# Query chunks of 512 columns with convolutions beside them, and 65-column arrays in a four-layer convolution and state-space network

## The reference

```python
# layer 0 (xf is the input plus its frequency-gated copy)
x_flat = xf.reshape(b, c, n).transpose(0, 2, 1)
q = (x_flat @ q_w + q_b)...                      # queries of all n pixels
xs = _conv(xf, sr_w, stride) + sr_b              # 8x8 stride 8, and 16x16 stride 16
...                                              # keys, values, attention, + x
# layer 2, its end
y = gaussian_smoothing_4d(dht_2d(out_ht) / (H * W))
mask = (jnp.abs(jnp.fft.fftfreq(W)) <= 0.25)     # 65 of 128 columns stay
return y * mask
# layer 3
xs = x.transpose(0, 2, 3, 1).reshape(1, -1, C)   # one sequence over all pixels
ys = mamba_fwd(xs, spa_...)                      # spatial branch
xe = x.transpose(0, 2, 3, 1).reshape(B * H * W, TOKEN, gcn)
ye = mamba_fwd(xe, spe_...)                      # spectral branch, each pixel by itself
spa = silu(group_norm(ys, ...)) + x
spe = x + silu(group_norm(ye, ...))
return spa * w[0] + spe * w[1] + x
```

## Time and profile before

| what | us |
|---|---|
| median of 3 runs (7890.61 to 7903.71) | 7898.19 |
| the profiled execution, device time | 7902.44 |
| its span | 7900.3 |
| patch stage, first load to the next stage's first load | 496.0 to 823.0 |
| attention | 893 to 2180 |
| spatial stage, first load of x to last result | 3547 to 5591 |
| spectral stage, first load of x to last result | 5601 to 7663 |
| merge stage | 7669 to 7900 |

### The profile page before, as it was taken

One profiled execution on the slowest core, in us unless ns is written; L12 is line 12 of the kernel. 1 busy time (PEld: TensorE's weight loads), 2 busy tenths in 40 slices (PEclk: granted clock), 3 DMA queues, 4 the chain that ended last, 5 costly groups with the idle time before them and its releaser, 6 DMA issues. The chain is left out here.

```text
span 7900.3 us, 122279 instructions
## 1 busy us (share of the span) xinstructions
PE 6835.9 (87%) x38266; PEld 3658.0 (46%) x38266; DVE 5843.1 (74%) x5708; ACT 4011.5 (51%) x6797; POOL 3601.8 (46%) x2430
## 2 busy tenths in 40 slices
PE   8967699999965499778999999999899999999970
PEld 7842333333244145662222222222477777777750
DVE  4652577777613385018999999999799999999975
ACT  4423366666612474015666666666455555555532
POOL 0100122222202000006777777777687787787860
PEclk9988799999977798668999999999899999999985
DMA  2252234334357333440000000000000000000016
GB/s 70 69 174 103 58 99 99 99 99 100 92 124 236 129 101 116 120 65 14 14 14 14 13 15 13 13 15 9 15 11 10 10 10 11 9 10 10 10 40 188
DMA packets 560486, 478.16 MB, mean 61 GB/s; under 512 B 181789, under 2 KB 486851, under 8 KB 551771
## 3 DMA queue, kind: packets, MB, share of 16 engines
q1 hardware_dynamic: 560155, 473.52, 21.9%
HBM read 306.97 MB, written 163.76 MB: 60 GB/s over the span
## 5 line engine op out<-in xcount | busy, mean ns | idle before, releaser
L2657 POOL TENSOR_TENSOR spe_hc<-spe_hs,spe_cu 128x1024 f32<-128x1024 f32 x552 | 1291.3, 2359 | 312.0 <-DVE spe_hs L2854 312.0
L2253 POOL TENSOR_TENSOR spa_hc<-spa_hs,spa_cr 128x966 f32<-128x966 f32 x592 | 1224.2, 2068 | 426.5 <-DVE spa_hs L2527 410.4
L2527 DVE TENSOR_TENSOR_SCAN spa_hs<-spa_p_d,spa_hs,spa_bx 128x483 f32<-128x483 f32 x1168 | 1359.4, 1204 | 0.0
L2854 DVE TENSOR_TENSOR_SCAN spe_hs<-spe_p_d,spe_bx 128x1024 f32<-128x1024 f32 x552 | 1233.8, 2275 | 106.3 <-ACT spe_p_d L2803 105.6
L2731 PE MATMUL spe_p_y<-spe_idt,spe_hc 128*128 128x128 f32 x8832 | 1039.7, 276 | 0.0
L2731 PEld LDWEIGHTS spe_p_y<-spe_idt,spe_hc 128*128 128x128 f32 x8832 | 1018.1, 193 | 0.0
L1048 DVE TENSOR_REDUCE attention_nm<-attention_p_s 128x2 f32<-128x640 f32 x1024 | 788.9, 812 | 259.6 <-PE attention_p_s L905 258.6
L2803 ACT ACTIVATE spe_p_d<-spe_p_d 128x896 f32<-128x896 f32 x552 | 474.1, 900 | 918.8 <-PE spe_p_d L2716 918.4
L1006 ACT ACTIVATE attention_pr<-attention_p_t 128x512 f32<-128x512 f32 x1280 | 710.6, 599 | 421.4 <-PE attention_p_t L928 288.7
L2438 ACT ACTIVATE spa_p_d<-spa_p_d,spa_av 128x483 f32<-128x483 f32 x1184 | 704.0, 634 | 410.7 <-PE spa_p_d L2310 408.5
L2310 PE MATMUL spa_p_d<-spa_du,spa_hot 32*128 32x483 f32 x2368 | 643.1, 618 | 58.4 <-DVE spa_hs L2527 49.2
(11 more groups left out here) (417 smaller groups left out, 10585.6 us busy)
## 6 DMA issues: line engine op xcount, KB each, us to landing
attention_qs<-scratch_qp SPq DMA_DIRECT2D x768, 64.0 KB, 2.8
attention_rc<-scratch_den SPq DMA_DIRECT2D x128, 256.0 KB
scratch_qp<-patch_parts SPq DMA_DIRECT2D x96, 256.0 KB, 2.0
spa_xt<-scratch_x SPq DMA_DIRECT2D x148, 121.5 KB, 2.6
front_xs<-in_x_dram SPq DMA_DIRECT2D x64, 256.0 KB, 3.0
scratch_xf<-front_out SPq DMA_DIRECT2D x128, 128.0 KB, 2.5
patch_x<-scratch_xf SPq DMA_DIRECT2D x8, 2048.0 KB, 18.7
attention_xs<-in_x_dram SPq DMA_DIRECT2D x128, 128.0 KB, 4.6
```

The lines of the kernel that those rows point to most:

```text
L2253: nc.gpsimd.tensor_tensor(hc[:, k % 8:k % 8 + 2, :], hs[:, k:k + 2, :], cr2[:, s % 2, :].unsqueeze(1).broadcast_to([128, 2, NA]), ALU.mult ...
L2527: nc.vector.tensor_tensor_scan(hs[:, k, v], p_d[k % 4][:, v], bx[:, k, v], 0.0 if start else hs[:, k, NA - 1:NA], ALU.mult, ALU.add).then_ ...
L2657: nc.gpsimd.tensor_tensor(hc[:, k, :, d, :].rearrange("p s d t -> p d s t"), hs[:, k % 2, d, :, :], rows, ALU.mult)\
L2854: nc.vector.tensor_tensor_scan(hs[:, k % 2, d].rearrange("p d s t -> p (d s t)"), p_d[h][:, :], bx[:, k % 2, d].rearrange("p d s t -> p (d ...
```

## The change

**Patch stage.** A query chunk is 512 columns, 64 chunks, with four buffers of PSUM, `qf`, `rest` and `parts`. SP waits for all three parts and stores them with one DMA of 3 x 512 values per row; `scratch_qp` has the chunk outside the part. The convolutions become a generator: from chunk 44 on, each query is followed by two of its 160 items (an item of the first is two matmuls of 512 columns, of the second one matmul of 256). In the second, even taps go to the first column strip and odd taps to the second, each over all images; the two sums are added at the end by two matmuls with stacked identities (`two`, loaded by two more DMAs).

**Attention.** The loads read the new layout.

**Layer 3.** The spatial stage computes as before on 69 columns, but stores only 65 of each row, joined (`full`), and copies its x from SBUF in the same way to a new array `xf2` (`keep_x`); the z projection waits for that copy (`x_kept`), since the load that waits for the projection overwrites its source. The spectral stage and the merge stage work on joined rows of 65: 4 x 128 x 65 / 512 = 65 chunks, and widths of 8320, 416 and 1040 instead of 8832, 368 and 1104.

```diff
-    HALF, QC, NQ, NX = HW // 2, 1024, B * HW // 2048, 8
+    HALF, QC, NQ, NX, NP, START = HW // 2, 512, B * HW // 1024, 8, 4, 44
...
-                for k, done in enumerate((first, second, third)):
+                for done in (first, second, third):
                     sp.wait_ge(done, u + 1)
-                    sp.dma_start(qv[k, :, b, cols], parts[:, u % 2, k]).then_inc(stored[u % 2], 16)
+                sp.dma_start(qv[:, u * QC // HALF, u % (HALF // QC), :], parts[:, u % NP].rearrange("p k n -> p (k n)")).then_inc(stored[u % NP], 16)
...
+                for t in range(32):
+                    for j in range(2):
+                        mm = nc.tensor.matmul(acc1[64 * j:64 * j + 64, :, :], wb[:, 0, t, :], x8[:, t // 8, t % 8, j], start=(t == 0), stop=(t == 31))
...
+                for t in range(128):
+                    i, e, j = t // 32 + 1, t // 16, t % 2
...
+                    mm = nc.tensor.matmul(acc2[64 * j:64 * j + 64, :, :], wb[:, i % 3, t % 32, :], x16[:, e, t % 16], start=(t < 2), stop=(t >= 126))
...
             for u in range(NQ):
                 query(u)
-            convolve(0, 0, 0, 4, True)
-            for i in range(4):
-                convolve(1, i + 1, 2 * i, 2 * i + 2, i == 3)
+                if u >= START:
+                    for i in range(2):
+                        next(rest_of)
...
+            for j in range(2):
+                mm = nc.tensor.matmul(acc3[64 * j:64 * j + 64, :, :], two[:, :], halves[:, j::2, :], start=True, stop=True)
...
-                if u >= 2:
-                    act.wait_ge(stored[u % 2], 48 * (u // 2))
+                if u >= NP:
+                    act.wait_ge(stored[n], 16 * (u // NP))
...
-                    src = qp[k, c.b, c.q].rearrange("(h d) n -> d h n", h=NH)[:, :, c.cols]
+                    src = qp[c.b, c.q].rearrange("(h d) m k n -> d h m k n", h=NH)[:, :, c.cols, k, :]
...
-                sp.dma_start(ys[:, bass.ds(c * NA, NA)], res[:, s % 2, :]).then_inc(stored[s % 2], 16)
+                sp.dma_start(ys[:, bass.ds(c * NF, NF)], full(res[:, s % 2, :])).then_inc(stored[s % 2], 16)
+
+            def keep_x(c, s, r):
+                sp.wait_ge(x_in[s], 32 * r + 32)
+                sp.dma_start(xf2[:, bass.ds(c * NF, NF)], full(xt[0:C, s, 3:3 + NA])).then_inc(x_kept[s], 16)
...
-            stream(sp, NC, UA, HEAD, 4, (0, next_load), (3, store))
+            stream(sp, NC, UA, HEAD, 4, (0, keep_x), (0, next_load), (3, store))
...
             def project_z(c, s, r):
-
+                pe.wait_ge(x_kept[s], 16 * r + 16)
...
-    NC, UE, HEAD = LX // GP, 4, 9
+    NC, UE, HEAD = LF // GP, 4, 9
...
-    K = H * KEPT
+    K = H * FULL
```

More of the change, by code:

```diff
@@ L613, in patches_and_queries @@
         bq_ = st.sb("bq", [128, 1])
[L614 to L618, removed]
+        two = st.sb("two", [128, C])
+        halves = st.sb("halves", [128, B, NK2])
+        qf = st.sb("qf", [128, NP, QC])
+        rest = st.sb("rest", [128, NP, QC])
+        parts = st.sb("parts", [128, NP, 3, QC], BF16)
+        p_q = [st.ps(f"p_q{s}", [128, QC]) for s in range(NP)]
+        acc1, acc2, acc3 = st.ps("acc1", [128, 2, NK1]), st.ps("acc2", [128, B, NK2]), st.ps("acc3", [128, 2, NK2])
         consts_in, x_in, w_in = st.sem("consts_in"), [st.sem(f"x_in{i}") for i in range(NX)], [st.sem(f"w_in{i}") for i in range(3)]
[L620 removed]
+        w_used, summed, copied, ready, xs_stored = (st.sem(n) for n in ("w_used", "summed", "copied", "ready", "xs_stored"))
         q_done, q_ready, first, rested, second, third = (st.sem(n) for n in ("q_done", "q_ready", "first", "rested", "second", "third"))
[L622 removed]
+        stored = [st.sem(f"stored{s}") for s in range(NP)]
         block = st.block()
[L625 to L627 removed]
         @block.sync
         def _(sp):
[L631 removed]
+            for dst, src in ((w[:, :], wq), (bq_[:, :], bq), (bs[:, :], bias), (two[0:C, :], ident[0:C, 0:C]), (two[C:128, :], ident[0:C, 0:C])):
                 sp.dma_start(dst, src).then_inc(consts_in, 16)
@@ L656, in _ @@
             sp.wait_ge(xs_stored, 16)
-            for s in range(2):
-                sp.wait_ge(stored[s], 48 * (NQ // 2))
+            for s in range(NP):
+                sp.wait_ge(stored[s], 16 * (NQ // NP))
         @block.tensor
@@ L687, in _ @@
+            pe.wait_ge(consts_in, 80)
+            rest_of = convolutions()
             for u in range(NQ):
                 query(u)
-            convolve(0, 0, 0, 4, True)
-            for i in range(4):
-                convolve(1, i + 1, 2 * i, 2 * i + 2, i == 3)
+                if u >= START:
+                    for i in range(2):
+                        next(rest_of)
+            for i in rest_of:
+                pass
+            pe.wait_ge(w_used, 1)
+            pe.sem_inc(summed, 1)
@@ L704, in read @@
                 act.wait_ge(q_ready, u + 1)
-                nc.scalar.activation(parts[:, u % 2, 0], qf[:, u % 2], ACT.Copy).then_inc(first, 1)
+                nc.scalar.activation(parts[:, n, 0], qf[:, n], ACT.Copy).then_inc(first, 1)
             def middle(u):
                 act.wait_ge(rested, u + 1)
-                nc.scalar.activation(parts[:, u % 2, 1], rest[:, u % 2], ACT.Copy).then_inc(second, 1)
+                nc.scalar.activation(parts[:, u % NP, 1], rest[:, u % NP], ACT.Copy).then_inc(second, 1)
@@ L2175, in rows, with full @@
             return t.rearrange("p (r w) -> p r w", w=KEPT)
+        def full(t):
+            return rows(t)[:, :, 0:FULL]
         def jumps(t):
```

114 lines of the change are left out of this document (63 added, 51 removed).

## The result

The changed kernel takes 7607.4 us (median of four runs, 7594.8 to 7609.6), the kernel before 7898.2. The ratio is 0.9629, with a 95% interval of 0.9612 to 0.9646. The prediction said 7699, range 7668 to 7730: right in sign, but 291 us went instead of 200, and the time lies outside the range.

What follows compares the result with a forecast made beforehand. Barrier-closed stages, each bound by whatever engine or transfer ends it: spectral 119.4, merge 9.7 and patch 71.5 saved, spatial 1.0 lost, 199.6 off 7902.4 gives 7702.8; that execution lay 4.2 above the median, so 7699 us, range 7668 to 7730.

Steps and rivals of the forecast that it cites:

- Spectral stage: Spectral loop: 65 chunks instead of 69 make 13 turns instead of 14, chunks otherwise unchanged; one turn goes, -119.4 us.
- the same 27.7 and 35 between them: Sign in the spectral stage's stores: 119 us fewer in total, spacing between stores and across the loop's end unchanged.
- Chunks don't pay: Rival, spectral stage: something that doesn't count chunks paces it, so its gain is missing: 7818 us; chance 0.02.
- Patch stage: Queries paced by ACT at 1.69 us a chunk, convolutions overlapped from query 44; next stage starts 71.5 us earlier.
- Merge: Merge stage: widths times 65/69 shorten loads, last statistics and final loop; -9.7 us, between 5.7 and 12.7.
- Spatial: Spatial stage: the copy of x stays hidden from PE's z projection; only the last store lands later, +1.0 us.
- Attention: Attention's query loads keep number and size; nothing changes if their landing stays near the median 2.8 us.
- the first case: Whole kernel: the forecast itself, 7699 us, chance 0.75, its own range given as 7687 to 7720.
- Stores pace the queries: Rival, patch stage: larger stores set the pace, 2.77 us a chunk, query 44 39 us later: 7738; chance 0.08.
- The second convolution halves: Rival, patch stage: both column strips stream at full rate, 56.7 us becomes 28: 7671; chance 0.07.
- Copies disturb DVE: Rival, spatial stage: small pieces leaving SBUF cost DVE's scans 1%, 20 us: 7719; chance 0.05.
- attention's loads late: Rival, attention: query loads landing beyond 5.7 us cost 128 us per us, at 7.8 giving 7968; chance 0.03.

Runs made afterwards that it cites:

- experiment 11: The changed kernel with both convolutions behind the last query, as in the kernel before: 7637.4 us in one run, patch stage 277.3.
- experiment 8: The changed kernel with the second convolution's taps not split over the strips, 256 matmuls of 128 columns: 7584.4 us in one run.

## Why the prediction was right and wrong

**Spectral stage: the step that failed.** "It isn't even: 27.7 us between most stores, 35.4 us across the loop's end", and then "What a chunk does is unchanged", so one turn of 119.4 goes. That much went. The step took the 35.4 as a property of the turn and priced only the one that disappears; it never asked what the 7.9 us over 28.0 was, though a quarter of every fourth chunk had no cause named. The views that answer it were there: the DVE waits (99.6 us, 26 times, all at boundaries), "issue" on PE 26 times, 236 packets of instructions for a program of 119 pieces. The runs showed that it depends on where the code lies, which every added or removed PE instruction ahead of it changes. Of the 93.6 us between the forecast's 199.6 and the 293.2 of the two spans, 95 are this row of the table; the others nearly cancel. The prediction's own sign, "the same 27.7 and 35 between them", failed: no 35 is left. "Chunks don't pay" was no rival worth having; "the boundary changes too" was the one that was missing.

**Patch stage: right mechanism, 8.7 short.** ACT is late next and not the store, as forecast. Its rows in after, and the last wait of PE for it, at query 44:

```profile
549.75 0.67 ACT L715 ACTIVATE patch_qf<-patch_p_q,patch_bq 128x512 f32<-128x512 f32 x1
550.52 0.63 ACT L719 ACTIVATE patch_parts<-patch_qf 128x512 bf16<-128x512 f32 x1
551.05 0.61 ACT L723 ACTIVATE patch_parts<-patch_rest 128x512 bf16<-128x512 f32 x1
551.57 0.67 ACT L715 ACTIVATE patch_qf<-patch_p_q,patch_bq 128x512 f32<-128x512 f32 x1
...
614.06 1.13 PE L664 MATMUL patch_p_q<-patch_x,patch_w 128*128 128x512 f32 x2 [0.69 <-ACT patch_qf L715]
```

1.82 us a chunk, not 1.69: 0.77 + 0.53 + 0.52 where I had 0.73 + 0.48 + 0.48. The two plain ones read SBUF, write bfloat16 and start 0.52 apart; my rows had ones that read PSUM and write float32, 0.48 apart, and no run separates the two differences. Over 36 chunks that is 4.7; the start, 548.70, was 1.4 better than 550.1. Query 44 came at 614.06 instead of 610.9. From there PE never waits, but needs 139.0 instead of 134.1 until 753.04:

```profile
686.88 1.12 PE L664 MATMUL patch_p_q<-patch_x,patch_w 128*128 128x512 f32 x2
687.94 3.87 PE L674 MATMUL patch_acc<-patch_x,patch_wb 128*64 128x512 f32 x8
691.74 1.12 PE L664 MATMUL patch_p_q<-patch_x,patch_w 128*128 128x512 f32 x2
...
699.05 53.99 PE L683 MATMUL patch_acc<-patch_x,patch_wb 128*64 128x256 f32 x244
753.62 0.44 PE L703 MATMUL patch_acc<-patch_halves,patch_two 128*64 128x128 f32 x4 [0.58 <-ACT patch_halves L733]
```

A query takes 1.06 from its start to the next record's, not the 0.92 of the convolution's stream: 20 x 0.14 = 2.8 us. The rest, 139.0 - 21.2 = 117.8 for the convolutions against 114.9 dense (experiment 11), is another 2.9 us. Both belong to the switches, as far as the rows tell. The first two records of a query start 0.53 apart, and so they did in before behind a wait (692.84 and 693.38), while the third followed at 693.80, 0.43 on. In a query of two records, with a switch ahead and behind, no record runs at the dense step. Together 5.7 us for 39 switches are 0.15 each. I had taken 0, on the strength of one row, and bounded it by 0.18; the truth lies near the bound. This is the mis-sized term of the stage, beside ACT's 0.13 a chunk, and the prediction's last sentence had named both as its ways to be wrong. The Trainium skill (TensorEngine Tiling (Array Packing), Key Properties) says that changing the tiling mode drains TensorE; the trace agrees in that each switch costs time, but no run shows that it is the drain. The tail was 6.2 where 6.5 was forecast.

**Merge: right,** 11.2 for 9.7. Statistics of the third and fourth array start at 7452.05 and 7472.41, 20.4 apart (forecast 20.3). A turn of the final loop went from 14.8 to 14.3 (7506.08 to 7520.41), 0.45 us for each of eight, 3.6 where I took 4.0. The last statistics took 10.24 and not 11.5: 20 instructions of 416 columns start 0.51 apart in the mean, as did 24 of 368, so their time went by their number and not by the width, as I had scaled it.

```profile
7452.05 10.03 DVE L3019 BATCH_NORM_STATS2 merge_bs<-merge_v 128x6 f32<-128x416 f32 x20 [10.15 <-DMA merge_v<-scratch_ye]
7472.41 10.24 DVE L3019 BATCH_NORM_STATS2 merge_bs<-merge_v 128x6 f32<-128x416 f32 x20 [10.33 <-DMA merge_v<-scratch_ye]
...
7506.08 0.76 DVE L3054 TENSOR_SCALAR merge_tx<-merge_xs,merge_at 128x1040 f32<-128x1040 f32 x1 [7.02 <-DMA merge_xs<-scratch_xf]
...
7520.41 0.76 DVE L3054 TENSOR_SCALAR merge_tx<-merge_xs,merge_at 128x1040 f32<-128x1040 f32 x1 [6.93 <-DMA merge_xs<-scratch_xf]
```

**Spatial: right.** The copies of x land 4.1 us after their issue (median, 24 in hand), and the z projection waits for none (what ended the idle time ahead of L2308, total us and times; "issue" is no semaphore):

```profile
  issue: 60.8, 74
  ACT spa_sg L2421: 3.1, 3
```

With the copies the stage took 2058.1 to 2062.3 in ten traces, without them 2057.9 to 2060.2 in three.

**Attention: right.** Median landing of the query loads 2.8, slowest 6.0, as in the earlier trace rows.

**The range.** The bounds that the prediction lists for the first case add up to 7699 + 16 + 4 + 7 = 7726, not 7720. It changes nothing in the outcome, since 7607 lies below every case it had.

**The rivals.** Stores pace the queries: no, ACT waits for a store once, at the start. The second convolution halves: no, 56.1 dense against 56.7, and experiment 8 says the same; no row shows the Trainium skill's up to 2x for matmuls of 64 columns (TensorEngine Tiling (Array Packing), Theoretical Speedup). Copies disturb DVE, attention's loads late: no.

## What to carry to other kernels

Before a stage's price is carried over, name every part of its period. A step that is longer only at a loop's boundary, with "issue" waits on one engine there and more instruction packets than the program has pieces, is code being fetched again; whether that happens depends on where the loop's code falls, so any edit ahead of it can switch it on or off and be credited or blamed for it. Compare stage by stage, not totals: half a change brought 158 us here, 103 of them in a stage that it didn't touch. A loop whose turn touches at most seven pieces wherever it starts, so one of at most six pieces' length by these rows, should not depend on luck; I haven't tried one.

## What I had not expected of the hardware

- PE keeps a turn of 6.43 pieces of 16.4 KB without fetching anything if it touches seven pieces, and fetches nine for every turn if it touches eight. The stall is 2.7 us when one fetch is waited for and 7.9 when two are, of which PE's own stops are 2.9 (38.0 / 13). Behind them the granted clock falls to its lower level (0.52 from 6176 to 6178, 0.50 until 6182, 0.77 until 6184, where it had been 1.00 up to the stops), which is 3.4 us of work lost, an estimate from these four figures. The remaining 1.6 isn't split.
- Records can be longer at the same pace. In the first trace of after DVE's scans in the spatial stage lasted 1404 ns, 1204 before, which reads like 17% more work on the engine that paces the stage. But two scans and a product started every 3.29 us in both:

```profile
4501.70 2.54 DVE L2556 TENSOR_TENSOR_SCAN spa_hs<-spa_p_d,spa_hs,spa_bx 128x483 f32<-128x483 f32 x2
4503.95 1.33 DVE L2542 TENSOR_TENSOR spa_bx<-spa_br,spa_p_u 128x952 f32<-128x952 f32 x1
4504.99 2.54 DVE L2556 TENSOR_TENSOR_SCAN spa_hs<-spa_p_d,spa_hs,spa_bx 128x483 f32<-128x483 f32 x2
```

  (before: 4501.10 and 4504.39), and the second trace of the same kernel has 1211. Why one execution's records were 0.2 us longer stays open.
- 160 semaphore increments on PE at a stage's start cost 17 us, 100 cost 7, 40 nothing. With 40, as without, PE's first matmul comes 7.5 us after SP's first constant, released by the last constant's load; with 100 and 160 it comes after 15.3 and 24.6 and waits for "issue". So a small number lies beside the loads.
